# Cross-attention on one core: three early projections of values moved into paired half rows beside the queries

## The chip, the cores and the metric

The kernel runs on one core of a Trainium2 chip. The metric is the device time of the whole program in microseconds; lower is better. The core has a matrix engine (PE, with its weight loads shown as PEld), a vector engine (DVE), an activation engine (ACT), GpSimd (POOL) and a queue that issues the transfers (SP). Each engine works through its own list of instructions in order, and they meet at semaphores.

## What is computed

A cross attention of 8 batches. Each has 1024 query rows and 64 context rows of width 512; there are 16 heads of 32.

```
Q = (query @ w_q.T).reshape(B, S, 16, 32).transpose(0, 2, 1, 3)
K, V = the same of the context with w_k and w_v
scores = jnp.einsum('bhqd,bhkd->bhqk', Q, K) / np.sqrt(32)
attn = jax.nn.softmax(scores, axis=-1)
ctx = jnp.einsum('bhqk,bhkd->bhqd', attn, V)
x = ctx.transpose(0, 2, 1, 3).reshape(B, S, 512) @ w_o.T + b_o + query
out = (x - mean(x)) * rsqrt(var(x) + 1e-5) * gamma + beta
```

## The kernel before

Each large operand is held as two parts, `_hi` (rounded by ACT) and `_lo` (the rest, by DVE or POOL), and each product is three passes: lo times hi, hi times lo, hi times hi. The rows are cut into 16 chunks of 512, and the query dimensions into 4 groups of 128, which makes 64 slots. Item n is one chunk and one group, so four heads of 512 rows.

What happens to item n on PE, in the names of the code:

- `project_queries(n)`: 12 matmuls (4 blocks of the contraction, 3 passes each) into the one bank `ps_q`. ACT makes `q_hi` of it (`queries_to_hi`), then DVE makes `q_lo` (`queries_to_lo`). `ps_q` is free for item n+1 once `q_lo` is done, which is the wait `queries_left`.
- `score(n)`: 3 steps of 2 half-row matmuls into `ps_s`, which holds three items in turn. It waits for `q_lo` of n, and for `c_raw` of n-3, which frees its place.
- DVE then turns the scores and takes their maximum (`turn_scores`, `half_maxima`, `fold_halves`), ACT negates it (`negate_max`), DVE turns it back (`turn_max`), SP fills `max_rows` by two transfers, and PE adds it in `subtract_max(n)`.
- ACT exponentiates, and PE makes context and sums in `combine_values(n)` (8 matmuls of 64 rows by 32 columns, which the timeline shows in two bursts). ACT turns the sums into an inverse, and DVE makes `c_raw` (`divide`).

The values of two batches at a time are `project_values(b2, ks)`: 4 blocks of 3 passes into the one bank `ps_o`, here in two calls of two blocks, `first_half` and `second_half`. ACT and DVE each copy one batch of it (`even_values`, `odd_values`), and the next projection into `ps_o` waits for both.

Slots 0 to 6 (`for t in range(OUT_LAG)`) fill the pipeline, with items t-2 to t+1 in them. From slot 7 on, a steady loop adds the output projection, and `project_both` runs it beside the queries in half rows: a matmul on partitions 0 to 63 for the one, and one on 64 to 127 for the other. Between its two halves stand `subtract_max` and the first step of a score. The first `project_both` waits for both copies of values 3, besides `q_lo` of item 7.

The order on every engine is written out by hand. On ACT a slot t of 3 to 6 reads: the logarithms for t-3, `negate_max(t - 1)`, the inverse, `exponentiate(t - 2)`, `context_to_hi(t - 3)`, `queries_to_hi(t + 1)`, a split of x, and in even slots `even_values` last. On DVE it reads: `turn_max(t - 1)`, `divide(t - 3)`, `queries_to_lo(t + 1)`, `turn_scores(t)`, `half_maxima(t)`, `fold_halves(t)`; `odd_values` stands after this in slots 2 and 4, and straight after `turn_scores` in slot 6. In slots 0 to 2 `queries_to_lo(t + 1)` and `turn_max(t)` follow `fold_halves(t)`.

Of the kernel before, what the change touches and what calls it, by code (L numbers as in the profile page):

```python
# [6 lines left out]
def cross_attention_kernel(nc, xT, x, ctxT, wqT, wkT, wvT, woT, b_o, gamma, beta, out):  # L7
# [3 lines left out]
    P = 128  # L11
# [5 lines left out]
    KT = DM // P  # L17
    CHUNK = 512
    CHUNKS = ROWS // CHUNK
    G = KT  # L20
# [12 lines left out]
    def wait(eng, sem, value):  # L33
        if value > 0:
            eng.wait_ge(sem, value)
# [5 lines left out]
    with ExitStack() as ctx:  # L41
        def sb(name, shape, dt, stack=ctx):
            return stack.enter_context(nc.sbuf_tensor(name, shape, dt))

        def sem(name):
            return ctx.enter_context(nc.semaphore(name))

        def tiled(names, dt, stack=ctx):
            return [sb(name, [P, KT, DM], dt, stack) for name in names]
# [9 lines left out]
        wq_lo, wo_lo = tiled(("wq_lo", "wo_lo"), fp32r)  # L59
        with ExitStack() as first:  # L60
            wv_lo, wv_hi = tiled(("wv_lo", "wv_hi"), fp32r, first)

        z, y = (sb(n, [P, 4, DM], fp32) for n in ("z", "y"))
        wq_hi, wo_hi = tiled(("wq_hi", "wo_hi"), fp32r)
# [14 lines left out]
        x_hi, x_lo = sb("x_hi", [P, 2, KT, CHUNK], fp32r), sb("x_lo", [P, 2, KT, CHUNK], fp32r)  # L79
# [13 lines left out]
        with ExitStack() as raw:  # L93
            wk_raw, _, ctx_raw = tiled(("wk_raw", "wk_hi_place", "ctx_raw"), fp32, raw)
        with ExitStack() as first:
            wk_lo, wk_hi, ctx_lo, ctx_hi = tiled(("wk_lo", "wk_hi", "ctx_lo", "ctx_hi"), fp32r, first)
# [14 lines left out]
        def ps(name, banks):  # L111
            return ctx.enter_context(nc.psum_tensor(name, [P, banks, 512], fp32))
# [3 lines left out]
        ps_s, ps_q, ps_o = ps("ps_s", 6), ps("ps_q", 1), ps("ps_o", 1)  # L116

        def scores(n):
            return ps_s[:, 2 * (n % 3):2 * (n % 3) + 2, :]
# [10 lines left out]
        def by_scalar(i):  # L130
# [14 lines left out]
        values_product, even_values_done, odd_values_done = (  # L145
            sem("values_product"), sem("even_values_done"), sem("odd_values_done"))
# [6 lines left out]
        q_product, q_copied, q_hi_done, q_lo_done = (  # L153
            sem(n) for n in ("q_product", "q_copied", "q_hi_done", "q_lo_done"))
# [1 line left out]
        upper_max_done, row_max_done, max_hi_done = sem("upper_max_done"), sem("row_max_done"), sem("max_hi_done")  # L156
        max_lo_done, max_turned_done = sem("max_lo_done"), sem("max_turned_done")
        max_rows_filled = [sem(f"max_rows_filled{s}") for s in range(2)]
        first_halves_done = sem("first_halves_done")
        shifted_done, exp_done = sem("shifted_done"), sem("exp_done")  # L160
        c_product, log_sum_done, inverse_done, c_raw_done = (
            sem(n) for n in ("c_product", "log_sum_done", "inverse_done", "c_raw_done"))
# [127 lines left out]
        def _(pe):  # L290
            def three_passes(dst, pairs, first=True, last=True):
                passes = [p for (l_hi, l_lo), (r_hi, r_lo) in pairs
                          for p in ((l_lo, r_hi), (l_hi, r_lo), (l_hi, r_hi))]
                for n, (lhs, rhs) in enumerate(passes):
                    mm = nc.tensor.matmul(dst, lhs, rhs, start=(first and n == 0),  # L295
                                          stop=(last and n == len(passes) - 1))
                return mm
# [6 lines left out]
            for k in range(KT):  # L304
                pe.wait_ge(ctx_lo_done, k + 1)
                pe.wait_ge(wk_lo_done, k + 1)
                for g in range(G):
                    dims = slice(g * P, (g + 1) * P)
# [6 lines left out]
            def queries_left(n):  # L315

                if n >= COPIED:
                    pe.wait_ge(q_copied, n - COPIED + 1)
                else:
                    wait(pe, q_lo_done, n + 1)  # L320

            def project_queries(n):
                c, g = divmod(n, G)
                queries_left(n - 1)
                if g == 0 and c > 0:
                    pe.wait_ge(x_lo_done, KT * (c + 1))
                for k in range(KT):
                    if n == 0:
                        pe.wait_ge(x_lo_done, k + 1)
                        pe.wait_ge(wq_lo_done, k + 1)  # L330
                    mm = three_passes(ps_q[:, 0, :], [
                        ((wq_hi[:, k, g * P:(g + 1) * P], wq_lo[:, k, g * P:(g + 1) * P]),
                         (x_hi[:, c % 2, k, :], x_lo[:, c % 2, k, :]))], first=(k == 0), last=(k == KT - 1))
                mm.then_inc(q_product, 1)

            def project_values(b2, ks):

                if ks[0] == 0:
                    wait(pe, even_values_done, 2 * b2)
                    wait(pe, odd_values_done, 2 * b2)  # L340
                keys = slice(b2 * P, (b2 + 1) * P)
                for k in ks:
                    if b2 == 0:
                        pe.wait_ge(wv_lo_done, k + 1)
                    mm = three_passes(ps_o[:, 0, :], [((ctx_hi[:, k, keys], ctx_lo[:, k, keys]),
                                                       (wv_hi[:, k, :], wv_lo[:, k, :]))],
                                      first=(k == 0), last=(k == KT - 1))
                if ks[-1] == KT - 1:
                    mm.then_inc(values_product, 1)

            def score(n, steps=range(3)):

                b, g, s = n // PER_BATCH, n % G, n % 2
                if steps[0] == 0:
                    wait(pe, q_lo_done, n + 1)
                    if n == 0:
                        pe.wait_ge(first_keys_hi_done, 4)
                        pe.wait_ge(first_keys_lo_done, 4)
                    elif n % PER_BATCH == 0:
                        pe.wait_ge(kbd_filled[b % 2], 16 * 8 * ((b + 1) // 2))  # L360

                    wait(pe, c_raw_done, n - 2)
                passes = ((kbd_lo, q_hi), (kbd_hi, q_lo), (kbd_hi, q_hi))
                for step in steps:
                    lhs, rhs = passes[step]
                    for pair in range(2):
                        rows = slice(64 * pair, 64 * (pair + 1))
                        mm = nc.tensor.matmul(scores(n)[:, pair, :], lhs[rows, b % 2, g, :], rhs[rows, s, :],  # L368
                                              start=(step == 0), stop=(step == 2))
                if steps[-1] == 2:  # L370
                    mm.then_inc(scores_done, 1)

            def subtract_max(n):
                if n == 0:
                    pe.wait_ge(select_filled, 16 * 8)
                pe.wait_ge(max_rows_filled[n % 2], 32 * (n // 2 + 1))
                for pair in range(2):
                    rows = slice(64 * pair, 64 * (pair + 1))
                    mm = nc.tensor.matmul(scores(n)[:, pair, :], select[rows, :], max_rows[rows, n % 2, :],  # L379
                                          start=False, stop=True, skip_group_check=True)  # L380
                mm.then_inc(shifted_done, 1)

            def combine_values(n):

                b, g = n // PER_BATCH, n % G
                pe.wait_ge(exp_done, n + 1)
                if n == 0:
                    pe.wait_ge(ones_done, 1)
                if n % PER_BATCH == 0:
                    pe.wait_ge(odd_values_done if b % 2 else even_values_done, 2 * (b // 2 + 1))  # L390
                for what in range(2):
                    for pair in range(2):
                        for head in range(2):
                            rows, col = slice(64 * head, 64 * (head + 1)), 64 * (what ^ head) + 32 * pair
                            mm = nc.tensor.matmul(context_and_sums(n)[col:col + DK, what, :],  # L395
                                                  ones[rows, :] if what else values[rows, b, g, pair, :],
                                                  probs[rows, n % 2, pair, :], start=True, stop=True)
                mm.then_inc(c_product, 1)
# [72 lines left out]
            first_half, second_half = range(KT // 2), range(KT // 2, KT)  # L471
# [3 lines left out]
            for t in range(OUT_LAG):  # L475
                if t < 3:
                    score(t)
                project_queries(t + 1)
                if t >= 3:
                    score(t)  # L480
                if t == 0:
                    project_values(0, second_half)
                else:
                    project_values((t + 1) // 2, first_half if t % 2 else second_half)
                if t >= 2:
                    combine_values(t - 2)
                if 1 <= t < OUT_LAG - 1:
                    subtract_max(t - 1)
# [538 lines left out]
```

## Time and profile before

| | |
|---|---|
| median of 3 runs | 532.32 us (532.07 to 532.65) |
| the profiled execution | 533.44 us, span 531.3 us |
| PE busy | 520.7 us, 98% of the span |
| POOL busy | 447.1 us, 84% |
| DVE busy | 431.2 us, 81% |
| ACT busy | 423.4 us, 80% |
| mean granted clock of PE | 0.997 of full |

The span runs from the first to the last instruction; the execution's own time is 2.14 us more than it. Busy shares are means over the whole program. The seven slots that the change touches end before 67 us of the 531.3.

### The profile page before, as it was taken

Reading aid. Unit: us, or ns where it says so; the run is one execution under the profiler, and the core shown is the slowest. Engines: PE = TensorE matmul, PEld = TensorE weight load, DVE = VectorE, ACT = ScalarE, POOL = GpSimd, SP = SyncE. Lnnn points to the kernel's source line nnn. Section 1 sums busy time; section 2 is a strip of 40 time slices with the busy share of each in tenths; the row PEclk is TensorE's granted clock in tenths of the full one; section 3 lists DMA queues with packets and bytes.
Section 4 is the critical chain, followed back from the end, with each engine's and each line's share of the span. In section 5 each row is a group of like instructions: output and inputs, shape, how many; then the busy total and the mean of one; then the engine's idle time right before and its main releaser. Section 6 shows DMA issues by size and latency. Waiting matters only on the chain.

```text
span 531.3 us, 12626 instructions
## 1 busy us (share of the span) xinstructions
PE 520.7 (98%) x4522; PEld 372.0 (70%) x4522; DVE 431.2 (81%) x877; ACT 423.4 (80%) x795; POOL 447.1 (84%) x387
## 2 busy tenths in 40 slices
PE   8999999999999999999999999999999999999994
PEld 6765577677677767777776777677777777777563
DVE  6886768878887788788878887878788878877897
ACT  6647767888888888888888888888888888877783
POOL 1735867999999999999999999999999999977956
PEclk9999999999999999999999999999999999999998
DMA  8943422333334433443244324342333332222123
GB/s 307 262 139 94 123 86 82 108 125 125 89 112 131 126 104 94 131 130 104 87 133 125 112 87 129 110 122 96 126 105 104 124 125 66 81 66 86 44 84 118
DMA packets 56750, 61.12 MB, mean 115 GB/s; under 512 B 29168, under 2 KB 29168, under 8 KB 56688
## 3 DMA queue, kind: packets, MB, share of 16 engines
q1 hardware_dynamic: 56688, 60.32, 36.4%
q8 instruction: 36, 0.59, 0.5%
q14 instruction: 26, 0.21, 0.1%
HBM read 39.58 MB, written 16.78 MB: 106 GB/s over the span
## 4 chain that ended last, share of the span: by engine, by line
PE 90%; DVE 4%; ACT 2%; issue 2%; DMA 1%; SPq 0%; DVEq 0%
PE ps_q L436 44%; PE ps_o L442 14%; PE ps_s L395 12%; PE ps_s L368 8%; PE ps_q L295 4%; PE ps_s L379 3%; PE ps_o L295 3%; PE ps_s L295 2%; DMA ctx_raw<-in_ctxT 1%; DVE stats L803 1%; DVE z L799 1%; ACT inverse L568 0%; DVE half_max L758 0%; DVE q_lo L713 0%; DMA max_rows<-max_turned 0%
## 5 line engine op out<-in xcount | busy, mean ns | idle before, releaser
L436 PE MATMUL ps_q<-x_hi,wq_lo 64*128 64x512 f32 x448 | 180.0, 402 | 0.2 <-issue 0.2
L442 PE MATMUL ps_o<-wo_hi,c_lo 64*128 64x512 f32 x448 | 180.2, 402 | 0.0
L442 PE MATMUL ps_o<-wo_hi,c_hi 64*128 64x512 f32 x448 | 173.9, 388 | 0.0
L436 PE MATMUL ps_q<-x_hi,wq_hi 64*128 64x512 f32 x448 | 173.8, 388 | 0.0
L436 PE MATMUL ps_q<-x_lo,wq_hi 64*128 64x512 f32 x448 | 173.3, 387 | 0.0
L442 PE MATMUL ps_o<-wo_lo,c_hi 64*128 64x512 f32 x448 | 173.1, 386 | 0.0
L436 PEld LDWEIGHTS ps_q<-x_hi,wq_lo 64*128 64x128 f32 x448 | 82.4, 184 | 56.3 <-DVE z L799 46.1
L936 POOL TENSOR_TENSOR c_lo<-c_raw,c_hi 128x512 fp32r<-128x512 f32 x63 | 81.6, 1296 | 42.5 <-ACT c_hi L525 42.5
L960 POOL TENSOR_TENSOR y<-y,beta_row 128x512 f32<-128x512 f32 x60 | 103.2, 1720 | 4.7
L436 PEld LDWEIGHTS ps_q<-x_hi,wq_hi 64*128 64x128 f32 x448 | 82.4, 184 | 13.3
L436 PEld LDWEIGHTS ps_q<-x_lo,wq_hi 64*128 64x128 f32 x448 | 82.7, 185 | 10.8
L943 POOL TENSOR_TENSOR x_raw<-x_raw,bias_row 128x512 f32<-128x512 f32 x64 | 85.7, 1341 | 0.0
L930 POOL TENSOR_TENSOR x_lo<-xT_raw,x_hi 128x512 fp32r<-128x512 f32 x60 | 77.5, 1293 | 9.2 <-ACT x_hi L525 9.2
L442 PEld LDWEIGHTS ps_o<-wo_lo,c_hi 64*128 64x128 f32 x448 | 82.7, 185 | 3.5
L442 PEld LDWEIGHTS ps_o<-wo_hi,c_hi 64*128 64x128 f32 x448 | 82.4, 184 | 3.2
L442 PEld LDWEIGHTS ps_o<-wo_hi,c_lo 64*128 64x128 f32 x448 | 82.4, 184 | 3.0
L789 DVE TENSOR_TENSOR c_raw<-ps_s,inverse 128x512 f32<-128x512 f32 x64 | 44.1, 689 | 49.7 <-ACT inverse L572 49.6
L614 ACT ACTIVATE probs<-ps_s 128x1024 f32<-128x1024 f32 x64 | 65.7, 1026 | 21.7 <-PE ps_s L379 21.7
L958 POOL TENSOR_TENSOR y<-y,gamma_row 128x512 f32<-128x512 f32 x60 | 77.9, 1298 | 5.9 <-ACT y L599 5.9
L753 DVE STREAM_TRANSPOSE turned<-ps_s 128x1024 f32<-128x1024 f32 x64 | 79.3, 1240 | 1.4 <-PE ps_s L368 1.4
L758 DVE TENSOR_REDUCE half_max<-turned 128x32 f32<-128x1024 f32 x64 | 77.5, 1210 | 0.3
L395 PE MATMUL ps_s<-probs,values 64*32 64x512 f32 x512 | 68.0, 601 | 0.1
(109 smaller groups left out, 1086.9 us busy)
## 6 DMA issues: line engine op xcount, KB each, us to landing
xT_raw<-in_xT SPq DMA_DIRECT2D x64, 256.0 KB, 3.0
x_raw<-in_x SPq DMA_DIRECT2D x64, 256.0 KB, 2.9
out<-y SPq DMA_DIRECT2D x64, 256.0 KB, 2.1
max_rows<-max_turned SPq DMA_DIRECT2D x128, 16.0 KB
ctx_raw<-in_ctxT SPq DMA_DIRECT2D x4, 256.0 KB, 5.5
wk_raw<-in_wkT SPq DMA_DIRECT2D x4, 256.0 KB, 5.7
wq_raw<-in_wqT SPq DMA_DIRECT2D x4, 256.0 KB, 6.5
wv_raw<-in_wvT SPq DMA_DIRECT2D x4, 256.0 KB, 7.4
```

Of the source, the lines that this page charges most:

```text
L295: mm = nc.tensor.matmul(dst, lhs, rhs, start=(first and n == 0), stop=(last and n == len(passes) - 1))
L395: mm = nc.tensor.matmul(context_and_sums(n)[col:col + DK, what, :], ones[rows, :] if what else values[rows, b, g, pair, :], probs[rows, n ...
L436: return nc.tensor.matmul(ps_q[:, 0, :], w[l][half, k, dims], x_[r][half, qc % 2, k, :], start=(half is lower and k == 0 and step == 0), s ...
L442: return nc.tensor.matmul(ps_o[:, 0, :], cx[l][half, k, tile], wo[r][half, k, :], start=(half is upper and k == 0 and step == 0), stop=(ha ...
L614: nc.scalar.activation(probs[:, n % 2, :, :], scores(n), ACT.Exp, scale=SCALE).then_inc(exp_done, 1)
L753: nc.vector.transpose(turned[:, :], scores(n).rearrange("p b r -> p (b r)")).then_inc(turned_done, 1)
L758: nc.vector.tensor_reduce(half_max[:, 0, :], turned[:, :].rearrange("p (b i) -> p b i", i=32), axis=AX.X, op=ALU.max).then_inc(half_max_do ...
L930: nc.gpsimd.tensor_tensor(x_lo[:, c % 2, k, :], xT_raw[:, k, :], x_hi[:, c % 2, k, :].bitcast(fp32), ALU.subtract).then_inc(x_lo_done, 1)
L936: nc.gpsimd.tensor_tensor(c_lo[c % 2][:, g, :], c_raw[:, :], c_hi[c % 2][:, g, :].bitcast(fp32), ALU.subtract).then_inc(c_lo_done, 1)
L943: nc.gpsimd.tensor_tensor(x_raw[:, i % 8, :], x_raw[:, i % 8, :], bias_row[:, :], ALU.add).then_inc(x_biased, 1)
L958: nc.gpsimd.tensor_tensor(y[:, s, :], y[:, s, :], gamma_row[:, :], ALU.mult).then_inc(scaled_done, 1)
L960: nc.gpsimd.tensor_tensor(y[:, s, :], y[:, s, :], beta_row[:, :], ALU.add).then_inc(y_done, 1)
```

## The change

A new function, `project_queries_and_values(n, b2)`, computes the queries of item n and all of values b2 together, in half rows: lower rows of the query with upper rows of the values, then the other way round. Its second half waits until the first half's last matmul is done, since both halves add into the same two banks. In slots 2, 4 and 6 it takes the place of `project_queries(t + 1)`; no other slot of 1 to 6 has a projection of values. Values 1, 2 and 3, whose first halves stood in slots 1, 3 and 5 and whose second halves in 2, 4 and 6, are now whole in slots 2, 4 and 6.

```diff
+            def project_queries_and_values(n, b2):
+                qc, g = divmod(n, G)
+                lower, upper = slice(0, 64), slice(64, 128)
+                dims, keys = slice(g * P, (g + 1) * P), slice(b2 * P, (b2 + 1) * P)
+                w, x_ = (wq_hi, wq_lo), (x_hi, x_lo)
+                cx, wv = (ctx_hi, ctx_lo), (wv_hi, wv_lo)
+                queries_left(n - 1)
+                pe.wait_ge(even_values_done, 2 * b2)
+                pe.wait_ge(odd_values_done, 2 * b2)
+                for half, other in ((lower, upper), (upper, lower)):
+                    if half is upper:
+                        pe.wait_ge(early_halves_done, b2)
+                    for k in range(KT):
+                        for step in range(3):
+                            l, r = ((1, 0), (0, 1), (0, 0))[step]
+                            begins, ends = k == 0 and step == 0, k == KT - 1 and step == 2
+                            mm_q = nc.tensor.matmul(ps_q[:, 0, :], w[l][half, k, dims], x_[r][half, qc % 2, k, :],
+                                                    start=(half is lower and begins), stop=(half is upper and ends))
+                            mm_v = nc.tensor.matmul(ps_o[:, 0, :], cx[l][other, k, keys], wv[r][other, k, :],
+                                                    start=(half is lower and begins), stop=(half is upper and ends))
+                    if half is lower:
+                        mm_v.then_inc(early_halves_done, 1)
+                mm_q.then_inc(q_product, 1)
+                mm_v.then_inc(values_product, 1)
...
             for t in range(OUT_LAG):
                 if t < 3:
                     score(t)
-                project_queries(t + 1)
+                if t >= 2 and t % 2 == 0:
+                    project_queries_and_values(t + 1, t // 2)
+                else:
+                    project_queries(t + 1)
                 if t >= 3:
                     score(t)
                 if t == 0:
                     project_values(0, second_half)
-                else:
-                    project_values((t + 1) // 2, first_half if t % 2 else second_half)
```

PE at the end of slot 1 and the start of slot 2, before. The rows into `ps_o` are the first half of values 1, L379 is `subtract_max(0)`, L368 is `score(2)`:

```order
L295 MATMUL ps_o<-wv_lo,ctx_hi 128x512
L295 MATMUL ps_o<-wv_hi,ctx_hi 128x512
L379 MATMUL ps_s<-max_rows,select 128x512 [waits max_rows_filled0,select_filled]
L379 MATMUL ps_s<-max_rows,select 128x512
L368 MATMUL ps_s<-q_hi,kbd_lo 128x512 [waits q_lo_done]
L368 MATMUL ps_s<-q_hi,kbd_lo 128x512
L368 MATMUL ps_s<-q_lo,kbd_hi 128x512 x2
L368 MATMUL ps_s<-q_hi,kbd_hi 128x512 x2
L295 MATMUL ps_q<-x_hi,wq_lo 128x512 [waits q_lo_done]
```

The same place after; the score is now L395, `subtract_max` L406, and L369 and L371 are the new function's two matmuls:

```order
L295 MATMUL ps_q<-x_hi,wq_hi 128x512
L406 MATMUL ps_s<-max_rows,select 128x512 [waits max_rows_filled0,select_filled]
L406 MATMUL ps_s<-max_rows,select 128x512
L395 MATMUL ps_s<-q_hi,kbd_lo 128x512 [waits q_lo_done]
L395 MATMUL ps_s<-q_hi,kbd_lo 128x512
L395 MATMUL ps_s<-q_lo,kbd_hi 128x512 x2
L395 MATMUL ps_s<-q_hi,kbd_hi 128x512 x2
L369 MATMUL ps_q<-x_hi,wq_lo 128x512 [waits odd_values_done,even_values_done,q_lo_done]
L371 MATMUL ps_o<-wv_hi,ctx_lo 128x512
```

The six matmuls into `ps_o` between the queries of item 2 and `subtract_max(0)` are gone from here, and `score(2)` with its wait for `q_lo` follows with nothing but `subtract_max(0)` between.

PE in slot 4 between the queries of item 5 and the values, before:

```order
L295 MATMUL ps_q<-x_hi,wq_hi 128x512
L368 MATMUL ps_s<-q_hi,kbd_lo 128x512 [waits c_raw_done,q_lo_done]
L368 MATMUL ps_s<-q_hi,kbd_lo 128x512
L368 MATMUL ps_s<-q_lo,kbd_hi 128x512 x2
L368 MATMUL ps_s<-q_hi,kbd_hi 128x512 x2
L295 MATMUL ps_o<-wv_hi,ctx_lo 128x512
L295 MATMUL ps_o<-wv_lo,ctx_hi 128x512
```

The same place after; L422 is `combine_values(2)`:

```order
L369 MATMUL ps_q<-x_hi,wq_hi 128x512
L371 MATMUL ps_o<-wv_hi,ctx_hi 128x512
L395 MATMUL ps_s<-q_hi,kbd_lo 128x512 [waits c_raw_done,q_lo_done]
L395 MATMUL ps_s<-q_hi,kbd_lo 128x512
L395 MATMUL ps_s<-q_lo,kbd_hi 128x512 x2
L395 MATMUL ps_s<-q_hi,kbd_hi 128x512 x2
L422 MATMUL ps_s<-probs,values 32x512 [waits exp_done]
L422 MATMUL ps_s<-probs,values 32x512 x3
```

The values no longer stand between `score(4)` and `combine_values(2)`; they are done before the score, inside the projection of the queries, whose last product comes that much later. The orders on the other engines are unchanged.

## Rows read from the trace of the kernel before

**Rows 1.** The page, chain of work that ended last: shares by engine.
```profile
PE 90%; DVE 4%; ACT 2%; issue 2%; DMA 1%; SPq 0%; DVEq 0%
```

**Rows 2.** Stretch of the steady loop: busy us (instructions) by engine, PEclk, DMA share, GB/s.
```profile
126.00:166.00 40.00, 40.00 (x386) 28.16 (x382) 33.59 (x69) 33.65 (x63) 37.32 (x32) 1.00 0.36 110
```

**Rows 3.** Timeline of PE, slots 3 and 4: start us, us, instruction.
```profile
39.22 0.50 PE L295 MATMUL ps_q<-x_hi,wq_lo 128*128 128x512 f32 x1
39.56 0.39 PE L295 MATMUL ps_q<-x_lo,wq_hi 128*128 128x512 f32 x1
...
41.86 0.39 PE L295 MATMUL ps_q<-x_hi,wq_hi 128*128 128x512 f32 x1
42.18 0.51 PE L368 MATMUL ps_s<-q_hi,kbd_lo 64*128 64x512 f32 x2
42.52 0.40 PE L368 MATMUL ps_s<-q_lo,kbd_hi 64*128 64x512 f32 x2
...
43.08 0.50 PE L295 MATMUL ps_o<-wv_hi,ctx_lo 128*128 128x512 f32 x1
43.42 0.40 PE L295 MATMUL ps_o<-wv_lo,ctx_hi 128*128 128x512 f32 x1
...
44.66 0.63 PE L395 MATMUL ps_s<-probs,values 64*32 64x512 f32 x4
...
45.12 0.61 PE L395 MATMUL ps_s<-probs,values 64*32 64x512 f32 x4
...
45.68 0.50 PE L379 MATMUL ps_s<-max_rows,select 64*128 64x512 f32 x2
46.11 0.50 PE L295 MATMUL ps_q<-x_hi,wq_lo 128*128 128x512 f32 x1
```

**Rows 4.** Timeline of PE, first slot of the steady loop: half rows side by side.
```profile
67.13 0.39 PE L436 MATMUL ps_q<-x_lo,wq_hi 64*128 64x512 f32 x1
...
69.42 0.39 PE L436 MATMUL ps_q<-x_hi,wq_hi 64*128 64x512 f32 x1
...
69.65 0.42 PE L379 MATMUL ps_s<-max_rows,select 64*128 64x512 f32 x2
...
73.05 0.41 PE L368 MATMUL ps_s<-q_hi,kbd_hi 64*128 64x512 f32 x2
73.40 0.63 PE L395 MATMUL ps_s<-probs,values 64*32 64x512 f32 x4
```

**Rows 5.** Timeline, end of slot 1: values 1, the query part, `score(2)`.
```profile
30.85 0.39 PE L295 MATMUL ps_o<-wv_hi,ctx_lo 128*128 128x512 f32 x1
...
31.83 0.68 DVE L713 TENSOR_TENSOR q_lo<-ps_q,q_hi 128x512 fp32r<-128x512 f32 x1
...
32.64 0.43 PE L368 MATMUL ps_s<-q_hi,kbd_lo 64*128 64x512 f32 x2
```

**Rows 6.** Timeline from `turn_scores(4)` on DVE to `score(5)` on PE.
```profile
50.48 1.24 DVE L753 STREAM_TRANSPOSE turned<-ps_s 128x1024 f32<-128x1024 f32 x1
...
55.34 0.69 DVE L789 TENSOR_TENSOR c_raw<-ps_s,inverse 128x512 f32<-128x512 f32 x1
...
56.17 0.51 PE L368 MATMUL ps_s<-q_hi,kbd_lo 64*128 64x512 f32 x2
```

**Rows 7.** Timeline from the last query matmul of item 7 to the first `project_both`.
```profile
62.74 0.39 PE L295 MATMUL ps_q<-x_hi,wq_hi 128*128 128x512 f32 x1
...
64.46 1.24 DVE L753 STREAM_TRANSPOSE turned<-ps_s 128x1024 f32<-128x1024 f32 x1
...
65.73 0.89 DVE L722 COPY values<-ps_o 64x256 f32<-64x256 f32 x2
...
66.83 0.47 PE L436 MATMUL ps_q<-x_hi,wq_lo 64*128 64x512 f32 x1 [0.21 <-issue]
```

**Rows 8.** Timeline late in the program: from `max_turned` to the `subtract_max` that waited.
```profile
491.84 0.21 DVE L784 STREAM_TRANSPOSE max_turned<-max_hl 128x32 f32<-128x32 f32 x1
...
494.78 0.49 PE L379 MATMUL ps_s<-max_rows,select 64*128 64x512 f32 x2 [0.60 <-DMA max_rows<-max_turned]
```

More of the change, by code:

```diff
@@ L158, in cross_attention_kernel @@
         max_rows_filled = [sem(f"max_rows_filled{s}") for s in range(2)]
-        first_halves_done = sem("first_halves_done")
+        first_halves_done, early_halves_done = sem("first_halves_done"), sem("early_halves_done")
         shifted_done, exp_done = sem("shifted_done"), sem("exp_done")
```

## The prediction

> **What bounds the kernel now.** I read the shares of the chain of work first: 90% of it is PE [rows 1]. Then I read the steady loop by stretches: in 40 us PE is busy for all 40.00, and no other engine for more than 37.32 [rows 2]. So the loop runs at PE's pace, and whatever moves its start moves the end by as much; I see nothing in it that could take up a delay, or that would swallow a gain. The question is when the first `project_both` starts, now at 66.83 us [rows 7].
>
> Then I read the timeline before that. In slots 3 and 4 PE goes from the first query matmul of item 4 to that of item 5 in 46.11 - 39.22 = 6.89 us with no idle time [rows 3]. PE looks like the bound there too, but two of its waits are nearly spent. Values 1, first half, ran from 30.85 to about 32.3, and `q_lo` of item 2, which `score(2)` needs next, ended only at 31.83 + 0.68 = 32.51; the score started at 32.64 [rows 5]. And `c_raw` of item 2 ended at 55.34 + 0.69 = 56.03, with `score(5)` starting at 56.17 [rows 6], so that score already waited for DVE. The first `project_both` started 0.21 us after the copies of values 3, 65.73 + 0.89 = 66.62 [rows 7]. These three places decide the case.
>
> **Prices on PE.** Full-array matmuls follow each other by (41.86 - 39.56) / 10 = 0.23 us [rows 3]. A pair of half-row matmuls takes (69.42 - 67.13) / 10 = 0.229 us [rows 4]. So 24 pairs cost what 12 query and 12 value matmuls cost full, 5.5 us: pairing by itself gains nothing. What is saved is the changes between full rows and half rows. Before and after one, the steps are 42.18 - 41.86 = 0.32 and 42.52 - 42.18 = 0.34 [rows 3] in place of 0.23, together 0.20 us; half rows after half rows step by 69.65 - 69.42 = 0.23 [rows 4]. Going into `combine_values` costs the same from full rows (the last value matmul, about 0.33) as from a score (73.40 - 73.05 = 0.35 [rows 4]). I count nine changes fewer: one in slot 2, one in each of slots 3 and 5 (score to values), three in each of slots 4 and 6 (into the queries, to the score, to the values). That is 9 x 0.20 = 1.8 us.
>
> The Trainium skill, TensorEngine Tiling (Array Packing), section Key Properties, says that changing the tiling mode drains TensorE. The steps of 0.32 and 0.34 agree with it; by that rule alone the program would end about 1.8 us earlier, and it is the first rival below.
>
> **What is added on PE.** The second half waits for the first half's last matmul, three times. The trace has no wait of PE for its own matmul with nothing between. A matmul ends 0.39 after its start, and the start after a release by DVE came 0.14 or 0.21 us later [rows 6, 7]; I take 0.10, since it is the same engine. So the step is about 0.49 in place of 0.23, and as the first step after a change is 0.34 [rows 3], I add 0.11: 0.35 to 0.37 each, say 0.35. Bounds: nothing, if the wait is free (no gain is possible); 0.20, the price of a change of mode; 0.55, if a weight load (about 0.19, half of a matmul's 0.39) is exposed too. Over three waits the sum moves by -1.05, -0.45 or +0.6.
>
> **Slot 1 and 2.** The six value matmuls of slot 1 go, 1.37 us. But they covered the wait for `q_lo` of item 2. Neither that part nor anything ahead of it on ACT and DVE changes, so `score(2)` still starts at about 32.64 [rows 5], and PE is idle in their place. Slot 2 has the six back. Its sum: score 0.73 to the first pair (33.37); 23 steps of 0.229 and the half wait, 5.62 (last pair starts 38.99, ends 39.38); to `combine_values` 0.34; then 45.12 - 44.66 = 0.46, 45.68 - 45.12 = 0.56 and 46.11 - 45.68 = 0.43 to the queries of item 4 [rows 3]: 40.78. These need `q_lo` of item 3, which now comes after the pairs. From the last query matmul's end to `turn_scores`, which follows `q_lo`, it takes 64.46 - 63.13 = 1.33 us, and `q_lo` itself ends some 0.1 after that [rows 7]: 39.38 + 1.5 = 40.9. Before, it was 39.22 [rows 3]. **Later by 1.7 us** (six matmuls +1.4, half wait +0.35, `q_lo` +0.1, one change -0.2).
>
> **Slots 3 and 4.** Slot 3: queries 42.18 - 39.22 = 2.96, score 0.57 and 0.34 to `combine_values`, 0.46, 0.56, and 0.33 to half rows: 5.22, so the pairs of item 5 start at 46.12. Last pair: start 51.74, end 52.13. PE alone is then at the queries of item 6 at 51.74 + 0.23 + 0.46 + 0.34 + 0.46 + 0.56 + 0.43 = 54.22, where before it is at 53.01 or so (39.22 + two slots of 6.89): later by 1.2, so these two slots give back 0.5.
>
> **Slot 5, the place that turns it.** `score(5)` waits for `c_raw` of item 2. DVE gets there only after `turn_scores(4)`, the maxima, `odd_values(2)` and `turn_max(4)`: from 50.48 to the score at 56.17 it takes 5.69 us, of which DVE is busy nearly all [rows 6]. With the values inside the projection, item 5's queries end at 52.13, not in the slot's middle, and `turn_scores(4)` stands behind `q_lo` of item 5: 52.13 + 1.33 = 53.46. The score can start at 53.46 + 5.69 = 59.15. PE would be ready at 54.22 + 2.96 = 57.18, since the values that lay between score and sums are gone: a new wait of about 2.0 us. Queued behind it are `combine_values(3)`, `subtract_max(4)` and the pairs of item 7, so all is late. Against 56.17 the score is 3.0 us later.
>
> **Slot 6 and the loop's start.** From the score to the pairs of item 7: 0.57 + 0.34 + 0.46 + 0.56 + 0.33 = 2.26, so they start at 61.41, the last at 67.03, ending at 67.42. Then again `q_lo`, `turn_scores(6)`, `odd_values(3)`: 1.33 and 66.83 - 64.46 = 2.37 [rows 7], which gives 71.12. PE is ready at 67.03 + 0.23 + 0.46 + 0.34 + 0.46 + 0.57 = 69.1, another wait of 2.0 us. **The loop starts 71.12 - 66.83 = 4.3 us later.**
>
> Two things that I cost at nothing. `subtract_max(4)` needs `max_rows`: 494.78 - (491.84 + 0.21) = 2.73 us from the end of `turn_max` [rows 8]. `turn_max(4)` ends before `c_raw` of item 2 starts, near 58.3, so the transfers are there at 61.0, and PE comes to it at 59.15 + 0.57 + 0.34 + 0.46 + 0.56 = 61.08: covered by 0.1 us. If the transfers take 0.5 longer, that is added. `even_values(3)` on ACT ends near 69.3, before DVE's copy.
>
> **Sum.** +1.7 (slot 2), -0.5 (slots 3 and 4), +1.8 (score 5), +1.3 (slot 6): +4.3 us. Against the span it is 531.3 + 4.3 = 535.6; that execution took 533.44, 1.1 above the median, so I put the same difference on the median: 532.32 + 4.3 = 536.6, rounded down to 536.5, since the waits on the own matmul have more room below.
>
> **Rivals.**
> - *Faster: the mode changes decide.* PE stays busy, and 1.8 us go, 0 to 1.05 come back in half waits: 530.5 to 531.5. For it: PE has no recorded idle time in slots 3 and 4. It needs `score(5)` and `project_both` to be ready when PE is, that is DVE's 5.69 and 3.7 us to run beside something; the rows show them in one line behind the last query product. 4%.
> - *Same: the delay is taken up later.* If the loop had slack of 4 us, the end would stay near 532.3. Against it: PE 40.00 of 40.00 us [rows 2]. A half case, in which the waits for DVE are real and something ahead of 32.64 moves earlier, ends here too. 6%.
> - *Slower, but by 3 to 3.5 us: the half waits are free.* 535.5. 12%.
> - *Slower by 5 or more:* weights exposed at each half wait, and `max_rows` late in slot 5: 4.3 + 0.6 + 0.5, 537.7. 10%.
> - The sum as it stands, 536.0 to 537.2: 68%.
>
> **Numbers.** The range 535.3 to 537.5 takes in the bounds of the half wait and leaves out the two first rivals and the far end of the fourth. 0.2% of 532 us is 1.1 us, about what a measurement can tell here. Faster by more 4%, within 6%, slower 90%.
>
> **What would show it.** In the new trace: idle PE of about 1.3 us ahead of `score(2)`, which stays near 32.6; a step near 0.49 in the middle of each set of 24 pairs, and 0.23 from pairs to score; PE idle about 2 us ahead of `score(5)`, released by `c_raw`, and about 2 us ahead of the first `project_both`, released by the copies of values 3; that one at 71.1; a loop of the old pace after it. It is wrong if `score(2)` moves earlier, if DVE reaches `c_raw` of item 2 before 58 us, or if the loop makes up time.

## The result, and the profile after

The changed kernel takes 538.53 us (median of 5 runs, 537.78 to 539.38) against 532.32 us (5 runs, 532.07 to 532.71): a ratio of 1.0116, 95% interval 1.0105 to 1.0127. The direction was forecast; the size was not. The range ended at 537.5 us. The profiled execution took 538.01 us, with a span of 536.1, 4.8 us over that of before.

The page of the changed kernel, the engines' busy time and the chain of work that ended last:

```profile
PE 521.1 (97%) x4594; PEld 373.3 (70%) x4594; DVE 426.1 (79%) x877; ACT 423.3 (79%) x795; POOL 447.4 (83%) x387
...
PE 91%; DVE 5%; ACT 2%; issue 1%; DMA 0%; SPq 0%; ACTq 0%; DVEq 0%
```

PE's busy time is almost where it was (520.7 before), and its share of the span is lower: most of the time went into idle stretches. The timeline of the changed kernel, slot 2 on PE (start us, us, instruction, and in brackets idle time and what ended it); L395 is the score, its first line here `score(1)`:

```profile
26.81 0.50 PE L395 MATMUL ps_s<-q_hi,kbd_lo 64*128 64x512 f32 x2
...
32.28 0.50 PE L395 MATMUL ps_s<-q_hi,kbd_lo 64*128 64x512 f32 x2 [1.08 <-DVE q_lo L741]
...
35.58 0.39 PE L369 MATMUL ps_q<-x_hi,wq_hi 64*128 64x512 f32 x1
...
36.03 0.50 PE L369 MATMUL ps_q<-x_hi,wq_lo 64*128 64x512 f32 x1
...
36.37 0.39 PE L369 MATMUL ps_q<-x_lo,wq_hi 64*128 64x512 f32 x1
...
40.52 0.50 PE L295 MATMUL ps_q<-x_hi,wq_lo 128*128 128x512 f32 x1
```

Answering to [rows 5]: `score(2)` starts no earlier than before relative to the work ahead of it, and where values 1 stood, PE is idle for 1.08 us. (Up to `score(1)`, 26.81 against the 27.10 us below, this execution ran 0.3 ahead.) The wait between the halves shows as steps of 0.45 and 0.34 in place of 0.23 twice. The queries of item 4 start at 40.52, against 39.22 in [rows 3]; with the 0.3 that is 1.6 us later. `score(1)` in the execution of before:

```profile
27.10 0.50 PE L368 MATMUL ps_s<-q_hi,kbd_lo 64*128 64x512 f32 x2
```

Slots 4 and 5 of the changed kernel, timeline of PE and DVE, answering to [rows 6]:

```profile
51.31 0.39 PE L369 MATMUL ps_q<-x_hi,wq_hi 64*128 64x512 f32 x1
...
51.54 0.39 PE L395 MATMUL ps_s<-q_hi,kbd_lo 64*128 64x512 f32 x2
...
53.03 1.24 DVE L781 STREAM_TRANSPOSE turned<-ps_s 128x1024 f32<-128x1024 f32 x1
...
57.88 0.69 DVE L817 TENSOR_TENSOR c_raw<-ps_s,inverse 128x512 f32<-128x512 f32 x1
...
58.72 0.50 PE L395 MATMUL ps_s<-q_hi,kbd_lo 64*128 64x512 f32 x2 [1.91 <-DVE c_raw L817]
```

`turn_scores(4)` starts 53.03 - 51.70 = 1.33 us after the last query matmul's end (51.31 + 0.39), and `score(5)` 5.69 us after that, the same two stretches as before. Only now PE comes to the score 1.91 us early. From the pairs to the score, both half rows, the step is 51.54 - 51.31 = 0.23. Slot 6 and the loop's start, answering to [rows 7]:

```profile
66.58 0.39 PE L369 MATMUL ps_q<-x_hi,wq_hi 64*128 64x512 f32 x1
...
68.30 1.24 DVE L781 STREAM_TRANSPOSE turned<-ps_s 128x1024 f32<-128x1024 f32 x1
...
69.57 0.89 DVE L750 COPY values<-ps_o 64x256 f32<-64x256 f32 x2
...
70.66 0.46 PE L463 MATMUL ps_q<-x_hi,wq_lo 64*128 64x512 f32 x1 [2.00 <-DVE values L750]
```

The loop starts 3.8 us later than at 66.83, or 4.1 counted from `score(1)`. Then comes what the prediction did not have. PE by stretches behind that start (length of the stretch, PE's busy us and instructions in it, the granted clock, DMA share, GB/s):

```profile
70.00:71.00 1.00, 0.34 (x3) 1.00 0.00 0
71.00:72.00 1.00, 1.00 (x10) 0.77 0.00 0
72.00:74.00 2.00, 2.00 (x13) 0.50 0.00 0
74.00:75.00 1.00, 1.00 (x8) 0.52 0.00 0
75.00:76.00 1.00, 1.00 (x10) 1.00 0.00 0
```

Two idle stretches of 1.91 and 2.00 us lay in the 14 us ahead, and about 0.9 us after the second the granted clock fell to 0.50, that is to 1.2 GHz, and stayed there almost until 75. `subtract_max(5)` starts at 75.08, 4.42 us after the loop's start, where before it is 69.65 - 66.83 = 2.82 [rows 4, 7]. So this fall cost 1.6 us. Sum of this execution: -0.3 (before `score(1)`), +4.1, +1.6, and -0.6 in the 54 slots of the loop from `score(8)` to `score(62)`, which went at 7.619 us each in this execution and at 7.631 in the one of before: 4.8 us. The 0.6 may be no accident of that one execution: in the profiles of all ten kernels below that pair a slot, those 54 slots took 0.3 to 0.6 us less than before, and in the two that pair none 0.05 less and 0.1 more. The loop seems to give a little back, a hundredth of a microsecond per slot; no run shows why.

The mean clocks of all five runs, the profiled one among them, bear the fall out: three with 0.993 took 537.78 to 538.53 us, two with 0.990 took 539.06 and 539.38. The median holds one fall. That 0.990 stands for two falls is inferred, since no execution with it was profiled. A mean clock has to be read with care: in every profiled execution, that of before too, the clock also falls after the last matmul, where it costs PE nothing (before: the last matmul ends near 523.8 us, and the clock is at 0.50 from 528 us to the end at 531.3). With that part alone the profiled executions have means of 0.995 to 0.998.

### The profile page after: what moved, and what is told of

The parts are those of the page before. It is cut to its first block, busy times and chain, and to the rows that moved or that the text cites. A ratio compares the mean times of both kernels' runs of the same rounds, so it can differ in the third digit from the quotient of the medians.

```text
span 536.1 us, 12770 instructions
## 1 busy us (share of the span) xinstructions
PE 521.1 (97%) x4594; PEld 373.3 (70%) x4594; DVE 426.1 (79%) x877; ACT 423.3 (79%) x795; POOL 447.4 (83%) x387
## 3 DMA queue, kind: packets, MB, share of 16 engines
HBM read 39.58 MB, written 16.78 MB: 105 GB/s over the span
## 4 chain that ended last, share of the span: by engine, by line
PE 91%; DVE 5%; ACT 2%; issue 1%; DMA 0%; SPq 0%; ACTq 0%; DVEq 0%
PE ps_q L463 53%; PE ps_s L422 11%; PE ps_s L395 8%; PE ps_o L469 6%; PE ps_q L369 3%; PE ps_s L406 3%; PE ps_q L295 3%; PE ps_s L295 2%; PE ps_o L295 1%; PE ps_s L302 1%; DVE half_max L786 1%; DVE turned L781 1%; DVE stats L831 1%; DVE q_lo L741 1%; DVE z L827 1%
## 5 line engine op out<-in xcount | busy, mean ns | idle before, releaser
L988 POOL TENSOR_TENSOR y<-y,beta_row 128x512 f32<-128x512 f32 x60 | 105.7, 1761 | 4.7
L971 POOL TENSOR_TENSOR x_raw<-x_raw,bias_row 128x512 f32<-128x512 f32 x64 | 83.3, 1305 | 0.0
L422 PE MATMUL ps_s<-probs,values 64*32 64x512 f32 x512 | 68.0, 601 | 0.1
```

The source lines that it names most:

```text
L971: nc.gpsimd.tensor_tensor(x_raw[:, i % 8, :], x_raw[:, i % 8, :], bias_row[:, :], ALU.add).then_inc(x_biased, 1)
L988: nc.gpsimd.tensor_tensor(y[:, s, :], y[:, s, :], beta_row[:, :], ALU.add).then_inc(y_done, 1)
```

## The experiments

"Counted from `score(1)`" means from its start to the first matmul of the steady loop, 66.83 - 27.10 = 39.73 us before and 70.66 - 26.81 = 43.85 with the change. Each kernel was timed beside the kernel before on the same chip, and the ratios are to that: 532.5 us for the three single slots and the kernel filled ahead of the loop; 532.95 for copies of values 3 first, the two with the score between the halves, and the mode changes without pairing; 532.8 for the other four.

**One slot at a time.** The change in slot 2, 4 or 6 alone; the other slots have their halves of values as before.

```diff
-                if t >= 2 and t % 2 == 0:
+                if t in (2,):      # (4,) and (6,) in the two others
                     project_queries_and_values(t + 1, t // 2)
...
+                elif t not in (1, 2):      # (3, 4) and (5, 6)
+                    project_values((t + 1) // 2, first_half if t % 2 else second_half)
```

(Left out: the half wait inside the new function then counts only the pairings that are left.)

> Only slot 2 pairs its queries with a whole projection of values; slots 3 to 6 are as in the kernel before. Theory A (the six value matmuls of slot 1 covered the wait for q_lo of item 2, and come back in slot 2): PE idle 1.1 us ahead of score(2), the queries of item 4 and everything behind 1.7 us later, no other new wait, clock 0.997; 534.0 us. Rival B (slot 2 costs nothing, all of the loss is the two waits for DVE in slots 5 and 6): 532.3 us or a little less.

> Only slot 4 pairs, slots 1, 2, 5 and 6 are as before. Theory A (score(5) waits for c_raw of item 2, whose chain on DVE now starts after the late queries of item 5): PE idle about 2.0 us ahead of score(5), that score at 57.6 instead of 56.2, the end 1.4 us later, 533.7 us. If an idle time of 2 us is enough for the granted clock to fall to its lower level, another 1.6 us, 535.3 us. Rival B (mode changes decide): four changes fewer, one half wait more, 531.9 us.

> Only slot 6 pairs, slots 1 to 4 are as before. Theory A (the loop's first matmul waits for the copies of values 3 on DVE): PE idle about 2.0 us ahead of it, that matmul at 68.2 instead of 66.8, the end 1.4 us later if the clock stays: 533.7 us. If the clock falls after this one idle time alone, as it does in the changed kernel: 535.3 us. Rival B: four mode changes fewer and one half wait more: 531.9 us.

Measured: slot 2 alone 534.34 us (ratio 1.0032, 1.0020 to 1.0044); slot 4 alone 535.26 (1.0042, 1.0027 to 1.0058); slot 6 alone 533.9 (1.0036, 1.0022 to 1.0050). PE idle ahead of `score(2)` 1.12 us; ahead of `score(5)` 1.92; ahead of the loop 2.00, each only in its own kernel. Counted from `score(1)` the loop starts later by 1.56, by 2.8 (1.5 of it the clock), and by 1.34. The three waits are thus independent, and without the clock they add up to 1.6 + 1.3 + 1.3 = 4.2, against the whole kernel's 4.1. Theory A holds three times, B none. The three waits, each in its own kernel:

```profile
31.74 0.50 PE L395 MATMUL ps_s<-q_hi,kbd_lo 64*128 64x512 f32 x2 [1.12 <-DVE q_lo L743]
...
57.43 0.50 PE L395 MATMUL ps_s<-q_hi,kbd_lo 64*128 64x512 f32 x2 [1.92 <-DVE c_raw L819]
...
67.91 0.50 PE L463 MATMUL ps_q<-x_hi,wq_lo 64*128 64x512 f32 x1 [2.00 <-DVE values L752]
```

The two kernels with one idle stretch of 2 us also split their runs by the clock. Slot 4 alone: 533.58 to 533.76 us in three runs at 0.996, 535.26 to 536.08 in four at 0.992 or 0.993. Slot 6 alone: 533.47 to 533.90 in four at 0.995 or 0.996, 535.33 to 535.60 in three at 0.992 or 0.993. The groups lie 2.0 and 1.9 us apart by their means, and one idle stretch of 2 us brings the fall in about half of these executions. In the profile of slot 4's kernel it comes about 1 us after `score(5)` at 57.43, and from there to `score(6)` PE takes 8.40 us in place of 6.89. PE by stretches:

```profile
54.00:57.00 3.00, 1.51 (x7) 1.00 0.00 0
57.00:59.00 2.00, 1.57 (x8) 0.85 0.11 16
59.00:61.00 2.00, 2.00 (x6) 0.50 0.91 279
61.00:62.00 1.00, 1.00 (x17) 0.60 0.56 205
```

Slot 2 alone, with 1.12 us idle, had no run under 0.995.

**The idle times filled.** The changed kernel with matmuls that do no work for the output (each product is overwritten) ahead of the loop, ahead of `score(5)`, or both.

```diff
+                    wait(pe, z_done, i)
+                    queries_left(n - 1)
                     if i == 0:
+                        for _ in range(9):
+                            nc.tensor.matmul(ps_q[:, 0, :], wq_hi[0:64, 0, 0:P], x_hi[0:64, 0, 0, :], start=True, stop=True)
                         pe.wait_ge(wo_lo_done, KT)
                         pe.wait_ge(even_values_done, 2 * KT)
                         pe.wait_ge(odd_values_done, 2 * KT)
-                    wait(pe, z_done, i)
-                    queries_left(n - 1)
...
                     project_queries(t + 1)
+                if t == 5:
+                    pe.wait_ge(even_values_done, 6)
+                    pe.wait_ge(odd_values_done, 6)
+                    for _ in range(6):
+                        nc.tensor.matmul(ps_o[:, 0, :], wq_hi[64:128, 0, 0:P], x_hi[64:128, 0, 0, :], start=True, stop=True)
```

> The changed kernel, with nine half-row matmuls into the free query bank, whose result is thrown away, in the idle time ahead of the first project_both, behind its wait for q_lo; the waits for the copies of values 3 stand behind them. The loop starts no earlier. Theory C (the half-speed stretch after that idle time costs 1.6 us by itself): granted clock full between 71 and 75 us, 1.6 us less than the changed kernel, 536.9 us. Rival D (the stretch is covered by other engines' waits, or the clock falls anyway): 538.5 us, no change.

> The changed kernel, with six half-row matmuls into the free values bank, result thrown away, in the idle time ahead of score(5); the idle time ahead of the loop stays. No start moves. The clock can now fall only behind the second idle time: mean clock never below 0.993, times of 537 (no fall) or 538.4 (one fall), never 539.

> The changed kernel with both idle times filled by thrown-away matmuls. If the falls of the clock are the part of the loss that the sum of waits leaves open: clock 0.995 or more in every run and 536.9 us. Rival: the clock falls by itself, and the time stays at 538.5 us.

Ahead of the loop: 537.03 us (1.0087, 1.0074 to 1.0100), no run under 0.995. Ahead of `score(5)`: 537.39 (1.0090, 1.0075 to 1.0105), two runs of five at 0.993 with 538.41 and 538.67, three at 0.996 or 0.997 with 536.43 to 537.39. Both: 536.76 (1.0077, 1.0065 to 1.0090), all at 0.995 or more. The added matmuls make nothing sooner: the loop starts 43.9 us after `score(1)` with the place ahead of `score(5)` filled, as in the changed kernel, and 44.0 with the place ahead of the loop filled, alone or with the other. (Ahead of `score(5)` PE is still idle for 0.46 us before the added matmuls.) PE by stretches with both filled:

```profile
56.00:60.00 4.00, 3.54 (x30) 1.00 0.10 16
68.00:72.00 4.00, 4.00 (x33) 1.00 0.12 41
72.00:76.00 4.00, 4.00 (x39) 1.00 0.02 4
```

The interval with both filled lies wholly under the changed kernel's 1.0105 to 1.0127. So 1.5 to 2.1 us of the loss, by the ratios, are the clock, and adding work that is thrown away makes the changed kernel that much faster. The rest, a ratio of 1.0077 or 4.1 us, are the waits.

**DVE's order.** The changed kernel with the copies of values 3 ahead of `turn_scores(6)`; and, apart from it, with the copies of values 2 behind `divide(2)`.

```diff
+                if t == OUT_LAG - 1:
+                    odd_values(t // 2)
                 turn_scores(t)
-                if t == OUT_LAG - 1:
-
-                    odd_values(t // 2)
```

```diff
                     divide(t - 3)
+                    if t == 5:
+                        odd_values(2)
                     queries_to_lo(t + 1)
...
-                if t % 2 == 0 and t < OUT_LAG - 1:
+                if t % 2 == 0 and t < 4:
                     odd_values(t // 2)
```

> The changed kernel, with the copies of values 3 on DVE in slot 6 ahead of turn_scores(6) instead of behind it. Theory A: the loop's first matmul comes 1.25 us earlier (69.4), but score(7) then waits 0.7 for c_raw of item 4; and with an idle time of 0.7 us instead of 2.0 the clock stays up, 1.6 us more: 2.1 us less in all, 536.4 us. Without the clock's part: 538.0 us.

> The changed kernel, with DVE's copies of values 2 moved from ahead of turn_max(4) to behind divide(2). If score(5) waits for exactly this chain on DVE, it starts 0.9 us earlier and its idle time falls from 1.9 to 1.0; the rest of the kernel follows 0.9 earlier (subtract_max(4) by 0.9 too, since turn_max(4) moves with it), the idle time ahead of the loop stays: 537.6 us, 0.9 under the changed kernel. If something else holds score(5): no change.

Copies of values 3 first: 536.45 us (1.0072, 1.0060 to 1.0085); four runs lie at 536.1 to 536.6 (0.995 to 0.997) and two at 538.0 and 538.1 (both 0.995). The gap is the size of one fall, and the idle time of 1.92 us ahead of `score(5)` is still there; but the profiled execution, 536.1 at 0.995, has no fall ahead of its end, so the mean clock does not settle it. The idle times on PE's timeline, where 0.7 was expected for the second:

```profile
69.62 0.47 PE L463 MATMUL ps_q<-x_hi,wq_lo 64*128 64x512 f32 x1 [0.84 <-DVE values L750]
...
73.37 0.50 PE L395 MATMUL ps_s<-q_hi,kbd_lo 64*128 64x512 f32 x2 [0.49 <-DVE c_raw L817]
```

The loop starts 1.1 us earlier counted from `score(1)`, about the 1.24 of the `turn_scores(6)` that the copies no longer stand behind, and `score(7)` waits in turn.

Copies of values 2 later: 537.65 us (1.0088, 1.0074 to 1.0102), the idle time ahead of `score(5)` 1.11 in place of 1.91, the loop 0.6 earlier. Three of its four runs are at 0.993 or 0.994 and 537.6 to 537.8, one at 0.995 and 536.61.

```profile
58.15 0.50 PE L395 MATMUL ps_s<-q_hi,kbd_lo 64*128 64x512 f32 x2 [1.11 <-DVE c_raw L817]
...
70.24 0.46 PE L463 MATMUL ps_q<-x_hi,wq_lo 64*128 64x512 f32 x1 [2.00 <-DVE values L750]
```

Both chains are on DVE where the prediction put them. A move gives about the time of the DVE work that is taken out of the chain (1.24 and 0.89 us), less what comes due behind it.

**Whole projections, unpaired.** Values 1, 2 and 3 whole in slots 2, 4 and 6, full rows, in their old place behind the score.

```diff
-                else:
-                    project_values((t + 1) // 2, first_half if t % 2 else second_half)
+                elif t % 2 == 0:
+                    project_values(t // 2, range(KT))
```

> The kernel before, with each of values 1, 2 and 3 whole in slots 2, 4 and 6 as in the changed kernel, but in full rows and still behind the score (in slot 2 behind the queries), not paired. If the two waits of 2 us come from the pairing, which puts the last query product and the score behind the values: score(4) and score(6) wait about 0.5 for c_raw, slot 2 still costs its 1.4, the loop's start is 2.0 late, clock full: 534.4 us. Rival: the waits come from gathering the values in the even slots, whichever way they are computed: 536 us or more.

Measured 535.01 us (1.0049, 1.0035 to 1.0063), with no run under 0.995, and the loop 2.7 us later counted from `score(1)`, where 2.0 was expected. PE's waits:

```profile
49.03 0.50 PE L368 MATMUL ps_s<-q_hi,kbd_lo 64*128 64x512 f32 x2 [0.91 <-DVE c_raw L789]
...
63.66 0.50 PE L368 MATMUL ps_s<-q_hi,kbd_lo 64*128 64x512 f32 x2 [0.98 <-DVE c_raw L789]
```

Slot 2 has the changed kernel's wait too (1.13 us ahead of `score(2)`). Gathering the values makes slots 3 and 5 short, and then `score(4)` and `score(6)` come before their `c_raw`, by 0.9 and 1.0 us where 0.5 was expected; no idle time is as long as 2 us. Two thirds of the 4.1 us are thus the gathering; the pairing adds the other 1.4, and the two long idle times on which the clock can fall.

**The score between the halves**, as the steady loop has it, with DVE's `turn_scores` and maxima of slots 4 and 6 ahead of `queries_to_lo` and the copies last; once for the whole change, once with slot 2 as before.

```diff
                     if half is lower:
                         mm_v.then_inc(early_halves_done, 1)
+                        if between is not None:
+                            score(between)
```

(Left out: the new argument, the call, and DVE's order.)

> The changed kernel, with the score of slots 4 and 6 between the two halves of the paired projection, and on DVE turn_scores, half_maxima and fold_halves of these slots ahead of queries_to_lo, the copies of values 3 last. If the waits for DVE come from where the pairs put the score and the queries, both shrink: score(5) 2.0 us earlier, the half waits of two slots gone (0.7), the loop 1.1 earlier, the clock at full (1.6): 5.4 us less than the changed kernel, 533.1 us. If pairing itself is what costs: above 537 us.

> As the kernel with the score between the halves, but slot 1 and 2 as in the kernel before, so that only slots 4 and 6 pair. Slot 2's 1.7 us go as well: 531.4 us, 0.9 under the kernel before (eight mode changes fewer, 1.6; a longer wait at the loop's start, 0.7). Rival: slot 2 is no cost of its own, 533 us.

Both missed: 537.74 us (1.0090, 1.0077 to 1.0103) and 536.41 (1.0065, 1.0053 to 1.0077), no run under 0.995; the loop starts 5.3 and 3.6 us later than before, counted from `score(1)`. PE's waits in the first:

```profile
49.31 0.50 PE L397 MATMUL ps_s<-q_hi,kbd_lo 64*128 64x512 f32 x2 [1.24 <-DVE c_raw L819]
...
58.49 0.50 PE L397 MATMUL ps_s<-q_hi,kbd_lo 64*128 64x512 f32 x2 [0.98 <-DVE c_raw L819]
...
65.03 0.50 PE L397 MATMUL ps_s<-q_hi,kbd_lo 64*128 64x512 f32 x2 [1.32 <-DVE c_raw L819]
...
71.29 0.46 PE L465 MATMUL ps_q<-x_hi,wq_lo 64*128 64x512 f32 x1 [1.52 <-DVE values L752]
```

I had looked at the wait of `score(5)` alone. The score in the middle of slots 4 and 6 comes before `c_raw` of items 1 and 3, which is the unpaired kernel's wait again. And `score(5)` waits although DVE had time: DVE was idle for 1.58 us ahead of `turn_max(4)`, which stands ahead of `divide(2)` and needs `negate_max(4)`; on ACT that stands behind the logarithms of item 2, and these behind the copies of values 2, which come with the late pairs. The wait moved from DVE's own work to the chain through ACT.

**Mode changes without pairing.** The kernel before, with the values of slots 3 to 6 ahead of the score, and on DVE the copies of values 3 ahead of `turn_scores(6)`.

```diff
                 project_queries(t + 1)
-                if t >= 3:
-                    score(t)
                 if t == 0:
                     project_values(0, second_half)
                 else:
                     project_values((t + 1) // 2, first_half if t % 2 else second_half)
+                if t >= 3:
+                    score(t)
...
+                if t == OUT_LAG - 1:
+
+                    odd_values(t // 2)
                 turn_scores(t)
-                if t == OUT_LAG - 1:
-
-                    odd_values(t // 2)
```

> The kernel before, unpaired, with the values of slots 3 to 6 ahead of the score instead of behind it, and the copies of values 3 ahead of turn_scores(6). Full rows follow full rows and half rows follow half rows: two mode changes fewer in each of four slots, 1.6 us, of which score(5) and score(7) give some 0.3 back: 531.0 us. If mode changes are no part of the time, 532.3 us; if DVE's chain from score to score is the bound, 532.3 or more.

Measured 532.93 us, ratio 0.9999 (0.9990 to 1.0008): no change, where 1.3 us less was expected. The loop starts 39.58 us after `score(1)`, 0.15 earlier, not 1.3. Two waits took the place of the mode changes, the first of them for a transfer:

```profile
52.23 0.49 PE L379 MATMUL ps_s<-max_rows,select 64*128 64x512 f32 x2 [0.84 <-DMA max_rows<-max_turned]
52.66 0.50 PE L295 MATMUL ps_q<-x_hi,wq_lo 128*128 128x512 f32 x1
...
59.34 0.50 PE L295 MATMUL ps_q<-x_hi,wq_lo 128*128 128x512 f32 x1
...
69.52 0.50 PE L368 MATMUL ps_s<-q_hi,kbd_lo 64*128 64x512 f32 x2 [0.46 <-DVE c_raw L789]
```

Slot 5, in which nothing waits, shows what the order itself saves: 59.34 - 52.66 = 6.68 us, against the 6.89 of a slot before. That is the 0.20 of one mode change, while the expectation had counted two per slot. With the values ahead, the change from score to values is gone; the one into the score stays, only it comes from the values. So the price of a change is confirmed, and the waits used up what four of them gave.

No kernel tried is faster than the one before.

## Why the prediction missed its size

- *The loop takes up nothing* held in the main: the delays of its start are in the end, less the 0.3 to 0.6 us by which the paired kernels' loops are shorter, which nothing in the prediction allowed for.
- *Prices on PE* held: pairs step by 0.23, pairs to score by 0.23. The Trainium skill, TensorEngine Tiling (Array Packing), section Key Properties, has a drain only at a change of mode, and the trace agrees: 0.23 from half rows to half rows. The half wait is 0.33 us more (0.45 + 0.34 - 2 x 0.23), where 0.35 was taken. The first rival had the price of a mode change right (0.20 forecast, 0.21 measured with the values ahead) and fell on its condition: `score(5)` and `project_both` were not ready when PE was.
- *Slot 2*: forecast 1.7 us later, measured 1.6 in the changed kernel and 1.6 alone, by the mechanism named.
- *Slots 3 and 4, slot 5*: forecast 3.0 us later at `score(5)` with 2.0 us idle; measured 2.8 (2.55, and 0.3 from the start) with 1.91. The 0.5 given back ahead of it came too: the queries of item 6 start 1.0 later where those of item 4 started 1.6 later. The stretches of 1.33 and 5.69 us came out to the hundredth.
- *Slot 6*: forecast 4.3, measured 4.1, idle time 2.00. The prediction's sign that it would be wrong, `c_raw` of item 2 before 58 us, shows by the raw time (57.88) and not with the 0.3 from the start (58.2); the chain behind it was the forecast one.
- **The step that failed** is the sum's last: it took PE's idle times as costing only their own length, and went from the loop's start straight to the end. The first 12 pairs behind the second idle time ran partly at half clock, 1.6 us more, and by the mean clocks every run had at least one such fall. 532.3 + 4.1 + 1.7 = 538.1 is the group of runs at 0.993; those at 539.1 to 539.4 lie 1.1 us above it, less than a full second fall. The filled kernels show the cause: with the waits as they were and work in the idle times, it is 536.76, near the 536.5 that was forecast. None of the rivals had it either. The one named "slower by 5 or more" came nearest in time (537.7), by two mechanisms of which neither came: the half wait was 0.33, and `subtract_max(4)` did not wait for `max_rows`.
- The prediction laid both waits of 2 us on the pairs. The unpaired kernel shows that gathering the values costs 2.7 us without them, by other waits.

Open is why the clock falls in some executions and not in others after the same idle time, what the two runs at 538 with the copies first had in them, since only their mean clock was recorded, and what shortens the loop of the paired kernels.

## What to carry to other kernels

Work that stands ahead of a wait is free; before it is moved, ask what PE does in its old place. In a pipeline that is this full, a place that waits for nothing today is late tomorrow: walk the chain of each semaphore from the instruction that is moved to the next one that needs it, on every engine, and also for the shorter slots. Where a change puts an idle time of about two microseconds into a busy matrix engine, add the price of a clock fall as a case with a chance of its own, and look at the spread of the runs.

## What I had not expected

The granted clock fell to 1.2 GHz after idle stretches of 1.9 to 2.0 us, in some executions of a kernel and not in others:

| kernel | idle stretches over 1.2 us | runs under 0.995 |
|---|---|---|
| changed | 1.91 and 2.00 | 5 of 5 |
| slot 4 alone | 1.92 | 4 of 7 |
| slot 6 alone | 2.00 | 3 of 7 |
| filled ahead of the loop | 1.91 | 0 of 4 |
| filled ahead of `score(5)` | 2.00 | 2 of 5 |
| copies of values 2 later | 2.00 | 3 of 4 |
| copies of values 3 first | 1.92 | 0 of 6, but two lie 1.8 us above the other four |
| filled in both places | none | 0 of 5 |

A fall cost 1.5 to 1.6 us in the profiles and 1.7 to 2.0 between the groups of runs (slot 4 alone, slot 6 alone, filled ahead of `score(5)`), close to the idle time itself. With 1.12 us idle (slot 2 alone), and with stretches up to 1.52 (the score between the halves, 9 runs), no run was under 0.995. Fifteen matmuls whose result is thrown away, put into the two idle stretches, gave a ratio of 1.0077 in place of 1.0116.
